# Layer 0 experts: owners loaded by fours, eight places for finished tiles, shared expert by four batches

## The chip, the cores and the metric

The kernel runs on one NeuronCore of a Trainium2 chip. The core has five engines that work side by side: TensorE (matrix products and transposes, PE in the rows; its weight loads are PEld), VectorE (DVE), ScalarE (ACT), GpSimd (POOL), and SyncE (SP), which issues most DMAs. TensorE reads SBUF and writes PSUM, eight banks of 128 x 512 floats; the other engines empty the banks. Engines wait for each other by semaphores. The metric is the time of one launch in microseconds of the device.

## What is computed

A decoder of four layers over 16 x 128 = 2048 tokens of width 256, each layer with attention, cross-attention and a feed-forward part. The change touches the feed-forward part of layer 0 alone, a mixture of 32 experts (inner width 128), of which each token takes 8, and a shared expert that all tokens take:

```python
aff = jax.nn.sigmoid(logits)
top_v, top_i = jax.lax.top_k(aff, K)
top_w = top_v / (jnp.sum(top_v, axis=-1, keepdims=True) + 1e-09)
...
shared = jnp.dot(silu(jnp.dot(x, Wg_s) + bg_s) * (jnp.dot(x, Wu_s) + bu_s), Wd_s) + bd_s
gate = silu(jnp.einsum('th,ehi->eti', x, Wg) + bg[:, None, :])
up = jnp.einsum('th,ehi->eti', x, Wu) + bu[:, None, :]
down = jnp.einsum('eti,eih->eth', gate * up, Wd) + bd[:, None, :]
routed = jnp.einsum('te,eth->th', w_full, down)
return (shared + routed).reshape(b, s, h)
```

## The kernel before

Only `l0_ffn` matters here. The 2048 tokens are 16 tiles of 128 rows, taken in three groups of 4, 8 and 4 tiles (`SIZES`). For each group the router finds for every token its 8 experts; GpSimd scatters the token's row 8 times into DRAM (`rows_dram`), sorted by expert and padded so that a tile of 128 rows holds rows of one expert only. That gives 63, 95 and 63 tiles, 221 in all (`ALL`). Which expert a tile belongs to, its owner, is known only at run time; a row `owner` in SBUF holds the numbers, and TensorE's sequencer loads them into registers (`values_load_multi_w_load_instructions`), since they address the expert's weights.

All engines then run one loop over units u, software-pipelined. SyncE reads tile m into one of four places of `tile_in`. `turn` (TensorE): two transposes of the tile; `copy` (ScalarE) brings them to `tileT`. `up`: a bias product and two products of 256 columns against the owner's gate and up weights, each fp32 product in two passes. `silu` on ScalarE, `multiply` on VectorE, `turn_hidden` (TensorE) transposes the hidden tile, `copy_hidden` (VectorE) brings it to `hiddenT`, `down` (TensorE) is one product of 256 columns. `take` (VectorE) copies the result to one of four places of `normed` (named `tile_out`), and SyncE writes that place to DRAM (`back_dram`). Before it uses a place, `take` waits for the semaphore `wrote` of the write four tiles earlier (line 2339); the copy itself (line 2340) waits for `downed`.

The order on TensorE in a round of u is turn(u + 3), up(u + 2), down(u), turn_hidden(u + 1). With every 24th tile (`BATCHED`), `turn` first loads the owners of the next 24 tiles (line 2109). VectorE's order is take(u), copy_hidden(u + 1), multiply(u + 2), and then what is due of `COMBINED`: when a token tile's 8 rows have come back by GpSimd's gathers (line 2050, gated by `out_taken`), VectorE adds them in 8 pieces, three to a unit (line 2360). That is done inside the loop for the 12 token tiles of groups 0 and 1; the last group is combined in a later stage.

The shared expert follows as 16 more units of the same loop, one for each token tile (`UNITS` = 16 + 221): a bias product (line 2130), two products with the tokens as stationary operand, silu, multiply, a transpose, a copy, a product of the routing weights with the experts' down biases (`bd`, line 2147) and the down product; VectorE adds the result to the tokens (line 2343). Then the next stage begins: its engines start, and SyncE issues its first loads, behind the end of this one.

Of the kernel before, what the change touches and what calls it, by code (L numbers as in the profile page):

```python
# [13 lines left out]
ALU = mybir.AluOpType  # L14
# [1833 lines left out]
def l0_ffn(k):  # L1848
# [15 lines left out]
    ALL = sum(TILES)  # L1864
    UNITS = BATCH + ALL
    BATCHED = 24
    rows_dram = k.routed
    back_dram = [nc.dram_tensor(f"expert_rows{g}", (TILES[g] * P, DIM), F32, kind="Internal").ap() for g in range(3)]
    k.last_rows = back_dram[2]
    with ExitStack() as stack:  # L1870
        wr, a = weights(k, stack, n + "Wr", KD, E)
        br, b = bias_row(k, stack, n + "br", E)
        bd = sb(k, stack, "bd", [P, DIM])
        shared_bias = sb(k, stack, "shared_bias", [P, DIM])
        before = sb(k, stack, "before", [P, P])
# [15 lines left out]
        xT = [k.xT, *(sb(k, stack, "xT", [P, KD, GT]) for _ in range(3))]  # L1891
        affinity, rest = sb(k, stack, "affinity", [P, 8, E]), sb(k, stack, "rest", [P, 8, E])
# [4 lines left out]
        mine, slots = sb(k, stack, "mine", [P, E * 8]), sb(k, stack, "slots", [P, E * 8])  # L1897
        is_it = sb(k, stack, "is_it", [P, GROUP * TOP, E])
# [10 lines left out]
        hiddenT = sb(k, stack, "hiddenT", [P, 2, INNER])  # L1909
        tile_out = k.normed  # L1910

# [17 lines left out]
        def out_bank(u):  # L1929
            return k.ps[:, 5 + u % 2, 0:DIM]  # L1930

        def turned_bank(m):
# [54 lines left out]
        with phase(k, "experts", names) as (block, s), ExitStack() as more:  # L1987
            for r in range(4):
                s[f"wrote{r}"] = more.enter_context(nc.semaphore(f"experts_wrote{r}"))
# [9 lines left out]
            def _(sp):  # L1999
# [6 lines left out]
                for m in range(ALL + 7):  # L2006
                    if m < ALL:
                        g = group_of(m)
                        if m == BEGIN[g]:
                            sp.wait_ge(k.scattered[g], 16 * TOP * SIZES[g])  # L2010
                        if m >= 4:
                            sp.wait_ge(s["tile_turned"], m - 3)
                        sp.dma_start(tile_in[:, m % 4, :], rows_dram[g][sl(m - BEGIN[g]), :]).then_inc(s[f"read{m % 4}"], 16)
                    if m >= 7:
                        j = m - 7
                        g = group_of(j)
                        sp.wait_ge(s["out_taken"], j + 1)
                        sp.dma_start(back_dram[g][sl(j - BEGIN[g]), :], tile_out[:, j % 4, :]).then_inc(s[f"wrote{j % 4}"], 16)
                for r in range(4):
                    sp.wait_ge(s[f"wrote{r}"], 16 * len(range(r, ALL, 4)))  # L2020

            @block.gpsimd
            def _(pool):
# [18 lines left out]
                for g in range(2):  # L2042
                    for r in range(4):
                        pool.wait_ge(s[f"wrote{r}"], 16 * len(range(r, BEGIN[g] + TILES[g], 4)))
                    for t in range(FIRST[g], FIRST[g] + SIZES[g]):
# [8 lines left out]
            def _(pe):  # L2054
# [41 lines left out]
                def weight(u, at, width):  # L2096
                    if not is_tile(u):
                        return experts[:, E, at:at + width]
                    return experts[:, bass.ds(expert_of[u], 1), at:at + width].rearrange("p o d -> p (o d)")

                def turn(m):
                    if m == 0:
                        for job in (("choose", 2), ("own", 1)):
                            job_taken(pe, job)
                    if m % BATCHED == 0:
                        count = min(BATCHED, ALL - m)
                        if m <= BEGIN[2] < m + count:
                            job_taken(pe, ("own", 2))
                        _, values = nc.values_load_multi_w_load_instructions(
                            owner[0:1, m:m + count], engines=[mybir.EngineType.PE], min_val=0, max_val=E - 1,  # L2110
                            skip_runtime_bounds_check_because="the owners are clamped to the last expert")
                        expert_of.update({m + j: value for j, value in enumerate(values)})
                    pe.wait_ge(s[f"read{m % 4}"], 16 * (m // 4 + 1))
# [6 lines left out]
                def up(u):  # L2120
                    if u >= 2:
                        pe.wait_ge(s["multiplied"], u - 1)
                    t = u - ALL
                    if is_tile(u):
                        if u == 0:
                            pe.wait_ge(s["weighted"], 16 * 5)
                        nc.tensor.matmul(gate_bank(u), one_hot[:, u:u + 1].broadcast_to([3 * E, P]), bias_parts[:, :], start=True, stop=False)
                        pe.wait_ge(s["tile_copied"], u + 1)
                    else:
                        nc.tensor.matmul(gate_bank(u), k.ident[:, 0:1].broadcast_to([P, P]), shared_bias[:, :], start=True, stop=False)  # L2130
                    for kt in range(KD):
                        x = tileT[:, u % 2, sl(kt)] if is_tile(u) else xT[t // GROUP][:, kt, sl(t % GROUP)]
                        last = nc.tensor.matmul(gate_bank(u), x, weight(u, 2 * kt * INNER, 2 * INNER), start=False, stop=kt == KD - 1)  # L2133
                    last.then_inc(s["upped"], 1)
# [7 lines left out]
                def down(u):  # L2142
                    if u >= 2:
                        pe.wait_ge(s["out_taken"], u - 1)
                    if not is_tile(u):
                        t = u - ALL
                        nc.tensor.matmul(out_bank(u), chosenT[t // GROUP][:, sl(t % GROUP)], bd[:, :], start=True, stop=False)
                    pe.wait_ge(s["hidden_copied"], u + 1)
                    nc.tensor.matmul(out_bank(u), hiddenT[:, u % 2, :], weight(u, 2 * KD * INNER, DIM), start=is_tile(u), stop=True).then_inc(s["downed"], 1)  # L2149

                for job in JOBS[:-7]:
                    make(job)
                for u in range(-3, UNITS):
# [5 lines left out]
                    if 0 <= u + 2 < UNITS:  # L2159
                        up(u + 2)  # L2160
                    if u >= 0:
                        down(u)
                    if 0 <= u + 1 < UNITS:
                        turn_hidden(u + 1)

            @block.scalar
            def _(act):
# [28 lines left out]
                def silu(u):  # L2196
# [11 lines left out]
                act.wait_ge(s["outered"], 1)  # L2208
                for u in range(-3, UNITS):
# [5 lines left out]
                    if 0 <= u + 2 < UNITS:  # L2215
                        silu(u + 2)

            @block.vector
            def _(dve):
# [115 lines left out]
                def take(u):  # L2335
                    dve.wait_ge(s["downed"], u + 1)
                    if is_tile(u):
# [3 lines left out]
                    else:  # L2341
                        t = u - ALL
                        v.tensor_tensor(k.x[:, t, :], out_bank(u), k.x[:, t, :], ALU.add).then_inc(s["out_taken"], 1)

# [41 lines left out]
                late = routing(2)  # L2386
                for u in range(-3, UNITS):
                    if u >= 0:
                        take(u)
                    if 0 <= u + 1 < UNITS:  # L2390
                        copy_hidden(u + 1)
                    if 0 <= u + 2 < UNITS:
                        multiply(u + 2)
                    if u in LATE_PIECES:
                        next(late, None)
                    for t, c in COMBINED.get(u, ()):
                        combine(t, c)
                for t in LEFT:
                    for c in range(TOP):
# [2531 lines left out]
def lay_out_rest(i, w):  # L4931
# [16 lines left out]
    w[n + "experts"] = np.concatenate([by_partition(np.concatenate([up, up_s[None]]), 2), down], axis=2).transpose(1, 0, 2)  # L4948
    w[n + "biases"], w[n + "shared_bias"] = np.tile(gate_and_up("b*", 1), (3, 1)), padded(row(gate_and_up("b*_s", 0)))
    w["numbers"] = np.broadcast_to(np.arange(32, dtype=np.float32), (P, 32))  # L4950
# [201 lines left out]
```

## Time and profile before

| | us |
|---|---|
| median of 3 runs (lowest, highest) | 3328.42 (3327.92, 3354.23) |
| span of the profiled execution | 3397.0 |
| tile loop of the layer 0 experts, first up to last up | 484.5 to 929.8 |
| shared expert, to the stage's last sum | to 970.8 |

The profile was taken in one execution of its own; its span is 68.6 us longer than the median run. In the rows below, a line such as L2133 is a line of the kernel before, `out<-in` are the program's names of what is written and read, `x4` is a count. A start and a duration stand in front; in square brackets stands how long the engine was idle before and what ended that. "issue" there means that nothing the profile shows was waited for. TensorE's matmuls overlap, and their ends are modelled: the pitch from start to start tells more than the duration.

### The profile page before, as it was taken

What the parts mean: (1) busy time and instruction counts of PE and PEld (TensorE: products, weight loads), DVE (VectorE), ACT (ScalarE), POOL (GpSimd) and SP (SyncE); (2) the same over time, 40 slices, a digit from 0 to 9 for tenths busy, and PEclk for the clock granted to TensorE, in tenths of its full rate; (3) what the DMA queues carried; (4) which work ended last, traced back from release to release, by engine and by line L of the source; (5) the groups of instructions that cost most, each with busy time, mean ns of one, the idle gap of its engine ahead of it and who ended that gap; (6) DMA issues with size and microseconds to landing.
All of it is one profiled execution on the core that took longest, in us unless ns stands there. A gap on an engine that the chain in (4) does not pass through costs nothing. (4 is left out here: it accounts for less than half of the span.)

```text
span 3397.0 us, 59298 instructions
## 1 busy us (share of the span) xinstructions
PE 3009.1 (89%) x20925; PEld 1857.6 (55%) x20929; DVE 2235.3 (66%) x4489; ACT 1822.0 (54%) x4182; POOL 1132.7 (33%) x1288
## 2 busy tenths in 40 slices
PE   7979759998887799987799989797799999999889
PEld 4656548877664556653467657454333333333567
DVE  6777645454546656667567747525589999996672
ACT  6967713333213344445566645211278888888554
POOL 3535555433432022215166653012111111221333
PEclk9999869999998999998889999898789999999989
DMA  9300156665530000022000032132401111110300
GB/s 301 133 9 2 47 203 210 207 188 173 158 101 26 26 1 1 1 73 85 33 1 1 1 118 106 64 109 88 113 1 20 20 21 20 21 20 1 125 13 25
DMA packets 158228, 243.61 MB, mean 72 GB/s; under 512 B 21298, under 2 KB 130482, under 8 KB 152482
## 3 DMA queue, kind: packets, MB, share of 16 engines
q1 hardware_dynamic: 144114, 202.05, 19.6%
q0 software_dynamic: 13824, 37.77, 3.4%
q8 instruction: 173, 2.83, 0.4%
q14 instruction: 117, 0.96, 0.1%
HBM read 132.64 MB, written 107.10 MB: 71 GB/s over the span
## 5 line engine op out<-in xcount | busy, mean ns | idle before, releaser
L4783 DVE TENSOR_REDUCE peaks<-ps 128x2 f32<-128x1024 f32 x512 | 617.6, 1219 | 64.8 <-PE ps L4727 63.0
L4820 ACT ACTIVATE attn<-ps 128x512 f32<-128x512 f32 x1024 | 558.8, 596 | 113.1 <-PE ps L4717 56.8
L4717 PE MATMUL ps<-queries,keys 50*128 50x512 f32 x1024 | 383.8, 455 | 0.0
L4727 PE MATMUL ps<-keys,queries 50*128 50x512 f32 x1024 | 370.2, 468 | 12.8 <-DVE peaks L4783 7.9
L4742 PE MATMUL ps<-attn,head_values 128*32 128x256 f32 x4096 | 332.3, 397 | 9.2 <-ACT output L4831 9.2
L4717 PEld LDWEIGHTS ps<-queries,keys 50*128 50x128 f32 x1024 | 157.6, 188 | 215.6 <-ACT attn L4820 197.5
L1239 POOL TENSOR_TENSOR attn_w<-attn_w,attn_share 128x512 f32<-128x512 f32 x128 | 131.7, 1050 | 373.0 <-DVE attn_share L1085 373.0
L2133 PE MATMUL ps<-experts,tileT 128*128 x884 | 232.0, 385 | 2.1 <-issue 2.1
L2340 DVE COPY normed<-ps 128x256 f32<-128x256 f32 x221 | 93.8, 424 | 202.9 <-PE ps L2149 106.8
L4742 PEld LDWEIGHTS ps<-attn,head_values 128*32 128x32 f32 x4096 | 82.3, 108 | 197.9 <-issue 108.6
L2194 ACT ACTIVATE tileT<-ps 128x256 f32<-128x256 f32 x221 | 84.6, 383 | 168.4 <-PE ps L2117 115.7
L2149 PE MATMUL ps<-experts,hiddenT 128*128 (+1 forms) x474 | 147.2, 392 | 25.1 <-DVE hiddenT L2349 21.1
L2133 PEld LDWEIGHTS ps<-experts,tileT 128*128 128x128 f32 x884 | 153.2, 193 | 19.4 <-issue 3.8
L4727 PEld LDWEIGHTS ps<-keys,queries 50*128 50x128 f32 x1024 | 147.5, 192 | 28.4 <-DVE peaks L4783 16.6
L2200 ACT ACTIVATE gate<-ps 128x128 f32<-128x128 f32 x237 | 65.8, 277 | 173.9 <-PE ps L2133 152.6
L1076 DVE TENSOR_REDUCE attn_peak<-ps 128x4 f32<-128x512 f32 x128 | 87.7, 685 | 95.9 <-PE ps L958 95.9
L4870 POOL CAST peak_parts<-peak 128x8 fp32r<-128x8 f32 x32 | 6.3, 197 | 407.4 <-DVE peak L4789 387.8
L2050 POOL DMA_INDIRECT rows<-expert_rows,index x96 | 91.0, 948 | 150.2 <-DMA expert_rows<-normed 60.9
L972 PE MATMUL ps<-xT,L_xattn_Wq 128*128 128x512 f32 x256 | 124.7, 610 | 7.7 <-ACT qT L1176 6.2
L2038 POOL DMA_INDIRECT routed_rows<-rows,index x96 | 96.3, 1003 | 87.7 <-DVE normed L2340 61.5
L2149 PEld LDWEIGHTS ps<-experts,hiddenT 128*128 128x128 f32 x474 | 86.8, 191 | 52.8 <-issue 41.1
L4885 POOL CAST queries<-peak_rows 2x128 fp32r<-2x128 f32 x256 | 73.5, 287 | 125.3 <-DVE peak_rows L4795 111.6
(733 smaller groups left out, 7164.5 us busy)
## 6 DMA issues: line engine op xcount, KB each, us to landing
tile_in<-routed_rows SPq DMA_DIRECT2D x244, 128.0 KB, 2.2
expert_rows<-normed SPq DMA_DIRECT2D x221, 128.0 KB
routed_rows<-zeros SPq DMA_DIRECT2D x2, 8064.0 KB, 48.1
experts<-in_L_ffn_experts SPq DMA_DIRECT2D x4, 3072.0 KB
routed_rows<-zeros SPq DMA_DIRECT2D x1, 12160.0 KB, 67.0
kT<-L_xattn_keys SPq DMA_DIRECT2D x8, 1024.0 KB
v<-L_xattn_values SPq DMA_DIRECT2D x8, 1024.0 KB, 8.7
experts<-in_L_ffn_experts SPq DMA_DIRECT2D x8, 1024.0 KB
```

The lines of the kernel that those rows point to most:

```text
L972: last = nc.tensor.matmul(query_bank, wq[:, kt, sl(4 * p + jj)], xT[g % 2][:, kt, :], start=kt == 0, stop=kt == KD - 1)
L1239: nc.gpsimd.tensor_tensor(w, w, share[:, n % 2, side, :].unsqueeze(2).broadcast_to([P, 4, P]), ALU.mult).then_inc(s_["scaled"], 1)
L2038: nc.gpsimd.indirect_dma_start(rows_dram[g][:, :], bass.IndirectOffsetOnAxis(index_of(slice(t, t + 1))[:, 0, c:c + 1], 0), rows[:, t, :], ...
L2050: nc.gpsimd.indirect_dma_start(rows[:, TOP * (t % 2) + c, :], None, back_dram[g][:, :], bass.IndirectOffsetOnAxis(index[:, t, c:c + 1], 0) ...
L2133: last = nc.tensor.matmul(gate_bank(u), x, weight(u, 2 * kt * INNER, 2 * INNER), start=False, stop=kt == KD - 1)
L2149: nc.tensor.matmul(out_bank(u), hiddenT[:, u % 2, :], weight(u, 2 * KD * INNER, DIM), start=is_tile(u), stop=True).then_inc(s["downed"], 1)
L2340: v.tensor_copy(tile_out[:, u % 4, :], out_bank(u)).then_inc(s["out_taken"], 1)
L4717: nc.tensor.matmul(bank(("score", n)), keys[pair % 2][rows, sl(kt)], queries[pair % 2][rows, sl(c, CHUNK)], start=True, stop=True).then_in ...
L4727: last = nc.tensor.matmul(k.ps[:, SB + p % PB, :], queries[pair % 2][rows, sl(t)], keys[pair % 2][rows, sl(c, CHUNK)], start=True, stop=True)
L4742: last = nc.tensor.matmul(mixed_bank[sl(strip, PAD), columns], head_values[:, u // CHUNKS % 2, strip % 2, 2 * part + strip // 2, :], attn[ ...
L4783: v.tensor_reduce(peaks[:, r % 2, i // CHUNKS, :, i % CHUNKS], k.ps[:, at:at + 2, :], AX.X, ALU.max).then_inc(s["maxed"], 1)
L4820: nc.scalar.activation(attn[:, n % RING, :], bank(("score", n)), ACT.Exp, scale=1.0 / 16.0).then_inc(s["read"], 1)
```

## The change

Three things are changed in `l0_ffn`.

Owners are loaded four at a time (`LOADED`), 56 loads for 221 tiles. The first stands ahead of the loop, each further one behind `down(u)`, for the tiles u + 4 to u + 7, and no longer in `turn`.

From tile 64 on (`WIDE`) finished tiles go to eight places in turn: the four of `normed` and four in the storage of `is_it`, which the router no longer needs by then. `take` then waits for the write eight tiles earlier. There are eight `wrote` semaphores.

The shared expert leaves the loop. It runs as four batches of 512 tokens, with the weights as stationary operand and the tokens streaming through, 512 columns at a time. The result is the hidden tile already transposed, so `turn_hidden` and `copy_hidden` fall away; a bias is now one value for each partition and enters in the silu and in VectorE's multiply. `shared_up(0)` stands ahead of the loop's last but one `down`, and `shared_up(i + 1)` ahead of the downs of batch i.

```diff
-    UNITS = BATCH + ALL
-    BATCHED = 24
+    LOADED = 4
+    WIDE = 64
...
-        tile_out = k.normed
+        outs = is_it[:, :, :].rearrange("p a e -> p (a e)")
+        shared_gate = [tile_in[:, 0:2, :].rearrange("p a d -> p (a d)"), ranked[:, :, :].rearrange("p a e -> p (a e)")]
+        shared_hiddenT = [tile_in[:, 2:4, :].rearrange("p a d -> p (a d)"), affinities[:, :, :, :].rearrange("p a t e -> p (a t e)")]
+
+        def tile_out(u):
+            return outs[:, sl(u % 4, DIM)] if u >= WIDE and u % 8 >= 4 else k.normed[:, u % 4, :]
+
+        def out_before(u):
+            return u - 8 if u >= WIDE + 8 else u - 4 if u < WIDE + 4 else -1
+
+        def written(engine, u):
+            engine.wait_ge(s[f"wrote{u % 8}"], 16 * (u // 8 + 1))
...
+                def owners(m):
+                    count = min(LOADED, ALL - m)
+                    if m <= BEGIN[2] < m + count:
+                        job_taken(pe, ("own", 2))
+                    _, values = nc.values_load_multi_w_load_instructions(
+                        owner[0:1, m:m + count], engines=[mybir.EngineType.PE], min_val=0, max_val=E - 1,
+                        skip_runtime_bounds_check_because="the owners are clamped to the last expert")
...
-                    if m % BATCHED == 0:
-                        count = min(BATCHED, ALL - m)
-                        if m <= BEGIN[2] < m + count:
-                            job_taken(pe, ("own", 2))
...
+                def shared_up(i):
+                    if i == 1:
+                        pe.wait_ge(s["multiplied"], ALL)
+                    if i >= 2:
+                        pe.wait_ge(s["shared_multiplied"], i - 1)
+                    for half in range(2):
+                        for kt in range(KD):
+                            last = nc.tensor.matmul(shared_bank(i, half), experts[:, E, sl(2 * kt + half)], xT[i][:, kt, :], start=kt == 0, stop=kt == KD - 1)
+                    last.then_inc(s["shared_upped"], 1)
+
+                def shared_down(t):
+                    pe.wait_ge(s["out_taken"], ALL + t - 1)
+                    out = out_bank(ALL + t)
+                    nc.tensor.matmul(out, chosenT[t // GROUP][:, sl(t % GROUP)], bd[:, :], start=True, stop=False)
+                    pe.wait_ge(s["shared_multiplied"], t // GROUP + 1)
+                    nc.tensor.matmul(out, shared_hiddenT[t // GROUP % 2][:, sl(t % GROUP)], experts[:, E, 2 * KD * INNER:COLS],
+                                     start=False, stop=True).then_inc(s["downed"], 1)
...
+                    if u == ALL - 2:
+                        shared_up(0)
                     if u >= 0:
                         down(u)
-                    if 0 <= u + 1 < UNITS:
+                    if is_tile(u + 4) and (u + 4) % LOADED == 0:
+                        owners(u + 4)
+                    if is_tile(u + 1):
                         turn_hidden(u + 1)
+                for i in range(GROUPS):
+                    if i + 1 < GROUPS:
+                        shared_up(i + 1)
+                    for t in range(GROUP * i, GROUP * i + GROUP):
+                        shared_down(t)
...
+                def shared_silu(i):
+                    act.wait_ge(s["shared_upped"], i + 1)
+                    if i >= 2:
+                        act.wait_ge(s["shared_multiplied"], i - 1)
+                    nc.scalar.activation(shared_gate[i % 2], shared_bank(i, 0), ACT.Silu, bias=shared_bias[:, 0:1]).then_inc(s["shared_silued"], 1)
...
-                        if u >= 4:
-                            dve.wait_ge(s[f"wrote{u % 4}"], 16 * (u // 4))
-                        v.tensor_copy(tile_out[:, u % 4, :], out_bank(u)).then_inc(s["out_taken"], 1)
...
+                    if out_before(u) >= 0:
+                        written(dve, out_before(u))
+                    v.tensor_copy(tile_out(u), out_bank(u)).then_inc(s["out_taken"], 1)
+
+                def shared_multiply(i):
+                    dve.wait_ge(s["shared_silued"], i + 1)
+                    if i >= 2:
+                        dve.wait_ge(s["downed"], ALL + GROUP * (i - 1))
+                    v.scalar_tensor_tensor(shared_hiddenT[i % 2], shared_bank(i, 1), shared_bias[:, 1:2], shared_gate[i % 2],
+                                           ALU.add, ALU.mult).then_inc(s["shared_multiplied"], 1)
...
+                shared_multiply(0)
+                shared_multiply(1)
+                for i in range(GROUPS):
+                    for t in range(GROUP * i, GROUP * i + GROUP):
+                        shared_take(t)
+                    if i + 2 < GROUPS:
+                        shared_multiply(i + 2)
```

On TensorE, around a load of owners in the middle of the loop, before (ISA is the step that computes a weight's address from the owner's register; `tile_in`, `tileT`, `hidden` and `hiddenT` are the tile and its hidden form, plain and transposed):

```order
L2149 MATMUL ps<-experts,hiddenT 128x256
L2140 MATMUL ps<-ident,hidden 128x128
L2109 TENSOR_LOAD owner
L2117 MATMUL ps<-ident,tile_in 128x128 x2
L2127 MATMUL ps<-bias_parts,one_hot 128x256
L2133 ISA
L2133 MATMUL ps<-experts,tileT 128x256
```

and in the changed kernel, at each fourth tile:

```order
L2157 MATMUL ps<-experts,hiddenT 128x256
L2121 TENSOR_LOAD owner
L2151 MATMUL ps<-ident,hidden 128x128
L2133 MATMUL ps<-ident,tile_in 128x128 x2
L2141 MATMUL ps<-bias_parts,one_hot 128x256
L2144 ISA
L2144 MATMUL ps<-experts,tileT 128x256
```

The load has moved from behind the hidden transpose to between the down product and that transpose.

On TensorE, one unit of the shared expert before (`xT` are the transposed tokens, `chosenT` the transposed routing weights):

```order
L2140 MATMUL ps<-ident,hidden 128x128
L2130 MATMUL ps<-shared_bias,ident 128x256
L2133 MATMUL ps<-experts,xT 128x256 x2
L2147 MATMUL ps<-bd,chosenT 128x256
L2149 MATMUL ps<-experts,hiddenT 128x256
```

and in the changed kernel from the loop's last hidden transpose on, with the first of the sixteen pairs of down (`tile_in` now holds the hidden tile of a batch):

```order
L2166 MATMUL ps<-xT,experts 128x512 x4
L2157 ISA
L2157 MATMUL ps<-experts,hiddenT 128x256
L2151 MATMUL ps<-ident,hidden 128x128
...
L2166 MATMUL ps<-xT,experts 128x512 x4
L2172 MATMUL ps<-bd,chosenT 128x256
L2174 MATMUL ps<-experts,tile_in 128x256
```

The bias products and the hidden transposes of the shared units are gone, and the ups stand in front of the downs by fours.

## Rows read from the trace of the kernel before

**Rows 1.** The head of the profile's page.
```profile
span 3397.0 us, 59298 instructions
```
**Rows 2.** Busy us (instructions) of PE, PEld, DVE, ACT, POOL, PEclk, DMA; then up (L2133).
```profile
520.00:800.00 280.00, 269.23 (x1524) 228.19 (x1523) 146.59 (x513) 100.19 (x304) 104.47 (x110) 1.00 0.63 194
800.00:936.00 136.00, 111.64 (x570) 87.96 (x569) 75.96 (x236) 34.81 (x112) 60.70 (x64) 0.96 0.57 168
...
L2133 PE MATMUL ps<-experts,tileT x884: 377/378/787, 484.5 to 930.5; 128*128 x177
```
**Rows 3.** Timeline of TensorE, a tile and then a load of owners: start, us, line.
```profile
578.26 1.03 PE L2133 MATMUL ps<-experts,tileT 128*128 x4
579.13 0.59 PE L2149 MATMUL ps<-experts,hiddenT 128*128 x2
579.56 0.27 PE L2140 MATMUL ps<-ident,hidden 128*128 128x128 f32 x1
...
580.00 1.03 PE L2133 MATMUL ps<-experts,tileT 128*128 x4
...
581.29 0.27 PE L2140 MATMUL ps<-ident,hidden 128*128 128x128 f32 x1
582.81 0.41 PE L2117 MATMUL ps<-ident,tile_in 128*128 128x128 f32 x2 [1.24 <-issue]
```
**Rows 4.** Waits of the stage: who waited for what; us in total, times, longest.
```profile
DVE normed L2340 <- remote: 21.8, 6, 3.9
...
PE ps L2117 <- issue: 10.3, 8, 1.5
```
**Rows 5.** Loads of owners: ns least/median/most, first and last start; all, two singly.
```profile
L2109 PEldq TENSOR_LOAD <-owner x10: 696/1864/2047, 463.5 to 919.5; - x10
...
L2109 PEldq TENSOR_LOAD <-owner x1: 1867/1867/1867, 580.8 to 580.8; - x1
...
L2109 PEldq TENSOR_LOAD <-owner x1: 696/696/696, 919.5 to 919.5; - x1
```
**Rows 6.** VectorE's waits for a place (L2339), all, then from 878 to 884.
```profile
L2339 DVEq EVENT_SEMAPHORE  x217: 21/21/2027, 501.4 to 934.2; - x109
...
L2339 DVEq EVENT_SEMAPHORE  x1: 21/21/21, 879.0 to 879.0; - x1
```
**Rows 7.** Timeline of that stall.
```profile
879.39 0.69 PE L2149 MATMUL ps<-experts,hiddenT 128*128 x2 [0.53 <-issue]
...
880.78 0.95 POOL L2050 DMA_INDIRECT rows<-expert_rows,index  x1 [0.30 <-issue]
...
880.99 0.38 ACT L2194 ACTIVATE tileT<-ps 128x256 f32<-128x256 f32 x1 [3.55 <-PE ps L2117]
...
883.22 0.42 DVE L2340 COPY normed<-ps 128x256 f32<-128x256 f32 x1 [3.87 <-remote]
```
**Rows 8.** Timeline of the last tile's up and of the end of the shared expert.
```profile
929.81 1.03 PE L2133 MATMUL ps<-experts,tileT 128*128 x4
...
968.24 0.70 PE L2149 MATMUL ps<-experts,hiddenT 128*128 128x256 f32 x2 [0.17 <-DVE hiddenT L2349]
...
969.65 0.70 PE L2149 MATMUL ps<-experts,hiddenT 128*128 128x256 f32 x2 [0.17 <-DVE hiddenT L2349]
970.39 0.42 DVE L2343 TENSOR_TENSOR x<-ps,x 128x256 f32<-128x256 f32 x1 [0.79 <-PE ps L2149]
```
**Rows 9.** Timeline of TensorE behind the load of five owners at 919.5.
```profile
920.50 0.27 PE L2140 MATMUL ps<-ident,hidden 128*128 128x128 f32 x1
920.61 0.38 PE L2117 MATMUL ps<-ident,tile_in 128*128 128x128 f32 x2
```
**Rows 10.** Like shapes elsewhere: 512-column passes, a multiply (busy, mean ns), a ScalarE function.
```profile
977.86 3.67 PE L3250 MATMUL ps<-xT,L_attn_W_q 128*128 128x512 f32 x8 [0.83 <-ACT xT L3320]
...
L3788 DVE SCALAR_TENSOR_TENSOR rows<-ps,factor,gate 128x512 f32<-128x512 f32 x32 | 23.1, 747 | 6.9 <-ACT gate L3724 5.2 <-PE ps L3678 0.7
...
L4820 ACT ACTIVATE attn<-ps 128x512 f32<-128x512 f32 x1024 | 558.8, 596 | 113.1 <-PE ps L4717 56.8
```

More of the change, by code:

```diff
@@ L1930, in out_bank, with shared_bank @@
             return k.ps[:, 5 + u % 2, 0:DIM]
+        def shared_bank(i, half):
+            return k.ps[:, 2 * (i % 2) + half, :]
         def turned_bank(m):
@@ L1987, in l0_ffn @@
         with phase(k, "experts", names) as (block, s), ExitStack() as more:
-            for r in range(4):
+            for m in ("shared_upped", "shared_silued", "shared_multiplied"):
+                s[m] = more.enter_context(nc.semaphore(f"experts_{m}"))
+            for r in range(8):
                 s[f"wrote{r}"] = more.enter_context(nc.semaphore(f"experts_wrote{r}"))
@@ L2042, in _ @@
                 for g in range(2):
-                    for r in range(4):
-                        pool.wait_ge(s[f"wrote{r}"], 16 * len(range(r, BEGIN[g] + TILES[g], 4)))
+                    for u in range(BEGIN[g + 1] - 8, BEGIN[g + 1]):
+                        written(pool, u)
                     for t in range(FIRST[g], FIRST[g] + SIZES[g]):
@@ L2096, in weight @@
                 def weight(u, at, width):
-                    if not is_tile(u):
-                        return experts[:, E, at:at + width]
                     return experts[:, bass.ds(expert_of[u], 1), at:at + width].rearrange("p o d -> p (o d)")
+                def owners(m):
[5 more added lines that the diff above has]
+                        skip_runtime_bounds_check_because="the owners are clamped to the last expert")
+                    expert_of.update({m + j: value for j, value in enumerate(values)})
                 def turn(m):
                     if m == 0:
-                        for job in (("choose", 2), ("own", 1)):
-                            job_taken(pe, job)
-                    if m % BATCHED == 0:
-                        count = min(BATCHED, ALL - m)
-                        if m <= BEGIN[2] < m + count:
-                            job_taken(pe, ("own", 2))
[L2109 to L2112, printed above, removed]
+                        job_taken(pe, ("choose", 2))
                     pe.wait_ge(s[f"read{m % 4}"], 16 * (m // 4 + 1))
@@ L2144, in down @@
                         pe.wait_ge(s["out_taken"], u - 1)
-                    if not is_tile(u):
-                        t = u - ALL
-                        nc.tensor.matmul(out_bank(u), chosenT[t // GROUP][:, sl(t % GROUP)], bd[:, :], start=True, stop=False)
                     pe.wait_ge(s["hidden_copied"], u + 1)
-                    nc.tensor.matmul(out_bank(u), hiddenT[:, u % 2, :], weight(u, 2 * KD * INNER, DIM), start=is_tile(u), stop=True).then_inc(s["downed"], 1)
+                    nc.tensor.matmul(out_bank(u), hiddenT[:, u % 2, :], weight(u, 2 * KD * INNER, DIM), start=True, stop=True).then_inc(s["downed"], 1)
+                def shared_up(i):
[14 more added lines that the diff above has]
+                                     start=False, stop=True).then_inc(s["downed"], 1)
                 for job in JOBS[:-7]:
                     make(job)
-                for u in range(-3, UNITS):
+                job_taken(pe, ("own", 1))
+                owners(0)
+                for u in range(-3, ALL):
                     for job in LATE:
@@ L2208, in _ @@
                 act.wait_ge(s["outered"], 1)
-                for u in range(-3, UNITS):
+                for u in range(-3, ALL):
                     for job in LATE:
@@ L2386, in _ @@
                 late = routing(2)
-                for u in range(-3, UNITS):
+                for u in range(-3, ALL):
                     if u >= 0:
                         take(u)
-                    if 0 <= u + 1 < UNITS:
+                    if is_tile(u + 1):
                         copy_hidden(u + 1)
-                    if 0 <= u + 2 < UNITS:
+                    if is_tile(u + 2):
                         multiply(u + 2)
@@ L4948, in lay_out_rest @@
     w[n + "experts"] = np.concatenate([by_partition(np.concatenate([up, up_s[None]]), 2), down], axis=2).transpose(1, 0, 2)
-    w[n + "biases"], w[n + "shared_bias"] = np.tile(gate_and_up("b*", 1), (3, 1)), padded(row(gate_and_up("b*_s", 0)))
+    w[n + "biases"], w[n + "shared_bias"] = np.tile(gate_and_up("b*", 1), (3, 1)), columns(gate_and_up("b*_s", 0))
     w["numbers"] = np.broadcast_to(np.arange(32, dtype=np.float32), (P, 32))
```

42 lines of the change are left out of this document (20 added, 22 removed).

## The prediction

> **What bounds the kernel now.** The change lies in one stage, the experts of layer 0, so I read that stage and not the shares of the whole span. The table by stretches comes first [rows 2]: from 520 to 800 us TensorE is busy 269.2 of 280 us at a granted clock of 1.00 (2.4 GHz), VectorE 146.6, ScalarE 100.2. TensorE bounds the tile loop. From 800 to 936 us it is busy 111.6 of 136, idle 24.4, at a clock of 0.96.
>
> The timeline of a tile is next [rows 3]: a row of TensorE work without a hole. Up starts at 578.26 and the next up at 580.00, 1.74 us later; four passes of up take 0.87 of it and two of down 0.43. From the first up (484.5) to the last (929.8) the loop takes 445.3 us [rows 2, 8], where 220 steps of 1.74 are 382.8. 62.5 us are lost; the change aims at two pieces of that, and at the shared expert.
>
> First piece: the load of owners. The eight waits on "issue" that TensorE's transposes of new tiles have sum to 10.3 us [rows 4], one for each of the eight loads of 24 values inside the loop. In the timeline the transposes start 1.52 us behind the hidden transpose (581.29 to 582.81) [rows 3]; without a load it is 0.11 (920.50 to 920.61) [rows 9]. A load costs 1.41, eight cost 11.3.
>
> Second piece: the copy of a finished tile to its place. The table of waits says that VectorE waited 21.8 us for "remote" ahead of that copy, in 6 waits [rows 4]. It reads like places that their writes have not left. But the instruction that waits for the place stands at L2339, apart from the copy: its median over 217 is 21 ns, and inside a stall of 3.87 us, at 879.0, it took 21 ns too [rows 6]. What came late there was TensorE's signal: down started at 879.39 and lasted 0.69, the copy began at 883.22; and ScalarE's copy of a turned tile, which waits for TensorE and for no place, is late in the same moments (idle 3.55) [rows 7]. GpSimd's gathers stand back to back beside it, 0.30 us apart. More places do not shorten that.
>
> Third piece: the shared expert, from the last tile's up (929.81) to the end of the last sum (970.39 + 0.42 = 970.81), 41.0 us [rows 8].
>
> **The change, part by part.**
>
> *Owners by fours.* Removed: 11.3 us, from above. Added: 55 loads inside the loop. Four values were never loaded; five took 696 ns and 24, in the load of [rows 3], 1867 (median 1864) [rows 5]. That is 62 ns for each further value, so four take 0.63 us. What of it shows depends on the work that is issued already. In [rows 3] the load starts at 580.8 [rows 5] and the issued work lasts until 581.4 (hidden transpose at 581.29 and 0.11): 0.6 us are covered. The load ends at 582.65, the next transpose starts at 582.81: 0.15 to start again. The new place is one step earlier, ahead of the hidden transpose; 0.11 less work is issued by then, but the load is reached about one step sooner, so I keep 0.6. Shown: 0.63 + 0.15 - 0.6 = 0.18 us. The load of five at 919.5 speaks for less: the transposes behind it follow at 920.61 without a hole [rows 9]. Of the 55 I take 45 as exposed; the others fall in tiles where VectorE holds TensorE up anyway (12 token tiles are combined inside the loop, each over three units). 45 x 0.18 = 8.1 us, and the edit is worth -11.3 + 8.1 = -3.2. Bounds: all covered, -11.3; nothing covered, 55 x 0.78 = 42.9, so +31.6. I stay at the low end because the nearest row, five values, shows no hole.
>
> A page of the Trainium skill speaks against this edit: "DMA: Bandwidth & Descriptors", section "Latency and other measured facts", gives a register load a floor of about 600 ns and says that loads are unrolled by four to spread it. The five-value row (696 ns) agrees. By the page, with each floor bare, 55 x 0.6 = 33 us would come in and the time would be 3342 us, an estimate; by the rows the issued work hides most of each load, and bare loads are a rival below.
>
> *Eight places from tile 64 on.* Removed: waits that take 21 ns. Worth 0. What covers them is the lag of four tiles, some 7 us, between a write and the reuse of its place; were a write later than that, each tile would wait for the rest. The write, its place in SyncE's queue and GpSimd's waits for a group's writes remain, under other semaphores. Bounds: 0, up to all that is lost from 800 to 936: 24.4 idle less two loads (2.8), and 4% of the clock (5.4), 27 us.
>
> *Shared expert.* Before: 41.0 us, as above. After, from the same up, on TensorE: up 0.86, down 0.43, hidden transpose 0.11, together 1.40. The first shared up. Down 0.43, transpose 0.11, the last down's wait for its hidden copy 0.87 (968.24 + 0.43 to 969.65 is 0.98 [rows 8], with a transpose of 0.11 in it), down 0.43, together 1.84. Three more shared ups. 16 pairs of down at 0.86, 13.8. The tail to the last sum 0.73 (969.65 + 0.43 to 970.81). A shared up is four products of 512 columns, eight passes; the nearest row has the same shape in the next stage, eight in 3.67 us [rows 10], at most 0.46 each with the modelled end of the last one in it; twice a pass of 256 columns (0.43 for two [rows 3]) is 0.43, and I take that: 3.44 an up, 13.8 for four. VectorE multiplies batches 1 to 3 ahead of the sums of the batch before. A signal of TensorE acts after 0.31 (969.65 + 0.43 to 970.39), a silu takes 0.60 on 512 columns, a multiply 0.75 [rows 10], the sum 0.42: with 0.05 between, the first sum ends 2.15 us behind a shared up, while TensorE wants its bank again after two pairs, 1.72. 0.43 is lost, three times: 1.3. Sum: 1.40 + 13.8 + 1.84 + 13.8 + 1.3 + 0.73 = 32.9 us. Gone are the bias product, the hidden transpose and the hidden copy of 16 units. Worth 32.9 - 41.0 = -8.1. Bounds: no wait, -9.4; silu and multiply bare behind all four ups (4 x 1.7 for 1.3), -2.6.
>
> *Sum.* -3.2 + 0 - 8.1 = -11.3 us. The profiled execution has a span of 3397.0 us [rows 1], 68.6 above the median of the runs (3328.42); no row says in which stage that lies. Against its own span the forecast is 3385.7, and the same 11.3 off the median is 3317.1 us. The next stage begins where this one ends (SyncE issues its first loads only then), so it moves by as much.
>
> **Rivals.**
>
> *The places matter (faster).* If the late signals come from traffic that the reuse of places keeps in step, loosening it could free the 27 us: 3290.1. For it: the stalls lie where gathers stand back to back. Against it: 21 ns at L2339 in the stall [rows 6], and ScalarE late as well [rows 7].
>
> *Bare loads (slower).* If a load is reached only when the array has run dry, each of 55 shows 0.63 + 0.15: -11.3 + 42.9 - 8.1 = +23.5, 3351.9. For it: down, right ahead of the load, waits for the hidden copy, so issue cannot run far ahead, and where that copy is late only down's own 0.43 covers. Against it: [rows 9]. It decides from 0.35 shown per load on ((11.3 + 8.1) / 55); below that the kernel is still faster.
>
> *Shared batches in single file.* Each batch pays silu and multiply bare: -2.6 for -8.1, 3322.6. Against it: the next batch's up is issued ahead of the downs of the one before.
>
> **How the numbers follow.** Forecast, with the single file inside it, 0.70; its own range is 3308 to 3330 (loads from all covered to 0.3 shown, the shared part between its bounds). Places 0.14. Bare loads 0.09. Something that no row shows 0.07. About 1% (33 us) is what a measurement of this kernel can tell from no change, and the forecast is within it. The places' case (3290.1) is just over it and makes, with a part of the unknown, the 0.16 for faster; bare loads end within it, so slower has 0.05 and the same 0.79. The range goes down to 3288 to hold the places, and up to 3338 to hold loads of which a good half is bare; outside stay the fully bare loads and the unknown.
>
> **What would show each step.** Right: 56 loads of some 0.63 us on TensorE's queue, holes under 0.25 us ahead of the hidden transpose, steps of 1.74 between; the wait for a place at 21 ns before and after tile 64; the stalls of some 3 us still there beside the gathers; the last tile's up to the last sum in 32 to 34 us, 512-column passes 0.43 apart. Wrong: four values take well over 0.7, or the hole is near 0.4; the stalls beside the gathers are gone; or this stage is shorter and a later one has grown by as much.

## The result, and the profile after

| | us |
|---|---|
| before, median of 8 runs (lowest, highest) | 3332.04 (3323.68, 3354.23) |
| changed, median of 8 runs (lowest, highest) | 3311.65 (3303.84, 3319.88) |
| ratio, 95% interval | 0.9929, 0.9912 to 0.9946 |
| forecast, range | 3317.1, 3288 to 3338 |

The changed kernel takes 20.4 us less between the medians, 0.6%, and 0.7% less by the ratio: within 1%, as forecast, and the interval leaves no doubt of the sign. The forecast was a gain of 11.3 us.

The profiled execution of the changed kernel took 3306.56 us, in line with its timed runs. Its span, 3304.7 us, is 92.3 us shorter than the one that [rows 1] shows, over four times what the timed runs give. The execution behind [rows 1 to 10] was a long one of its kernel, so I compare with a second profile of the kernel before, taken later, and come back to the first below.

The stage of the changed kernel by stretches (stretch, length, then busy us and instructions of PE, PEld, DVE, ACT, POOL; PEclk, DMA share, GB/s), the answer to [rows 2]:

```profile
520.00:800.00 280.00, 277.44 (x1583) 236.75 (x1582) 149.62 (x523) 104.35 (x315) 112.56 (x118) 1.00 0.65 203
800.00:884.00 84.00, 80.47 (x441) 65.02 (x440) 62.94 (x193) 29.12 (x88) 49.29 (x51) 1.00 0.74 218
```

From 520 to 800 us TensorE is idle 2.6 us, where it was 10.8 [rows 2]; behind 800 the clock is 1.00 and 3.5 of 84 us are idle. The tiles' up products now run from 477.2 to 883.9, 406.6 us.

The loads of owners (ns least/median/most, first and last start), and one of them singly, the answer to [rows 5]:

```profile
L2121 PEldq TENSOR_LOAD <-owner x56: 305/333/520, 453.9 to 880.8; - x56
...
L2121 PEldq TENSOR_LOAD <-owner x1: 332/332/332, 626.5 to 626.5; - x1
```

TensorE's timeline around that one (start, us, line), the answer to [rows 3]:

```profile
625.79 1.03 PE L2144 MATMUL ps<-experts,tileT 128*128 x4
626.65 0.59 PE L2157 MATMUL ps<-experts,hiddenT 128*128 x2
627.09 0.27 PE L2151 MATMUL ps<-ident,hidden 128*128 128x128 f32 x1
...
627.53 1.03 PE L2144 MATMUL ps<-experts,tileT 128*128 x4
```

A load of four takes 333 ns, not 630. It starts at 626.5, beside the products of down, and is over at 626.86; the hidden transpose follows down after 0.44 us and the next up after 1.74: no hole. In TensorE's waits of the stage the "issue" ahead of the transposes of new tiles, 10.3 us in [rows 4], is gone (who waited for what: us, times, longest):

```profile
PE ps L2157 <- DVE hiddenT L2401: 5.7, 16, 0.8
PE ps L2157 <- issue: 1.6, 10, 0.2
PE ps L2172 <- DVE x L2395: 0.2, 1, 0.2
```

The end of the stage, the answer to [rows 8]: the last tile's up, the first two shared ups, a bubble, the last down and the last sum.

```profile
883.86 1.03 PE L2144 MATMUL ps<-experts,tileT 128*128 x4
885.39 0.69 PE L2157 MATMUL ps<-experts,hiddenT 128*128 x2 [0.51 <-DVE hiddenT L2401]
...
886.03 3.60 PE L2166 MATMUL ps<-xT,experts 128*128 128x512 f32 x8
889.47 0.59 PE L2157 MATMUL ps<-experts,hiddenT 128*128 x2
...
890.97 0.69 PE L2157 MATMUL ps<-experts,hiddenT 128*128 x2 [0.80 <-DVE hiddenT L2401]
891.50 3.60 PE L2166 MATMUL ps<-xT,experts 128*128 128x512 f32 x8
...
896.23 0.59 PE L2174 MATMUL ps<-experts,tile_in 128*128 128x256 f32 x2
897.00 0.70 PE L2172 MATMUL ps<-bd,chosenT 128*128 128x256 f32 x2 [0.17 <-DVE x L2395]
...
916.50 0.59 PE L2174 MATMUL ps<-experts,affinities 128*128 128x256 f32 x2
917.13 0.42 DVE L2395 TENSOR_TENSOR x<-ps,x 128x256 f32<-128x256 f32 x1 [0.44 <-PE ps L2174]
```

From 883.86 to 917.55 are 33.7 us, for 41.0 before and 32.9 forecast.

### The profile page after: what moved, and what is told of

Same layout as the page of the kernel before. It is cut to its first block and busy times, and to the rows that moved or that the text cites. A ratio compares the mean times of both kernels' runs of the same rounds, so it can differ in the third digit from the quotient of the medians.

```text
span 3304.7 us, 59090 instructions
## 1 busy us (share of the span) xinstructions
PE 2969.0 (90%) x20849; PEld 1829.3 (55%) x20849; DVE 2226.6 (67%) x4461; ACT 1823.7 (55%) x4170; POOL 1133.1 (34%) x1288
## 5 line engine op out<-in xcount | busy, mean ns | idle before, releaser
L2157 PE MATMUL ps<-experts,hiddenT 128*128 x442 | 134.8, 387 | 7.4 <-DVE hiddenT L2401 5.7
L2384 DVE COPY normed<-ps 128x256 f32<-128x256 f32 x144 | 61.1, 424 | 117.1 <-PE ps L2157 114.6
L4322 POOL TENSOR_TENSOR lasting<-lasting,pairs 128x512 f32<-128x512 f32 x64 | 81.1, 1281 | 82.0 <-ACT lasting L4247 82.0
```

## The experiments

**A second profile of the kernel before.** No edit.

> The kernel before, unchanged, profiled a second time. In the profile shown, its tiles take 445.3 us from the first tile's up products to the last tile's, 38.7 us more than in the changed kernel's profile, of which only about 11 us are holes at the loads of the owners; the rest are some ten stalls of about 3 us in tiles 160 to 215. Theory A (the stalls were the profiled execution's own, not the kernel's): this profile has the tiles in 415 to 420 us, a span about 3310 to 3330 us, the stretch 800 to 936 us without stalls, and the holes at loads again: 1.9 us nine times, 0.7 us once. Rival B (the four places for finished tiles make the stalls): 440 to 447 us of tiles again, with some eight to ten stalls of about 3 us after tile 160.

Its span is 3321.2 us. The stage in two stretches (columns as above):

```profile
520.00:800.00 280.00, 268.03 (x1514) 228.34 (x1512) 143.06 (x500) 99.91 (x302) 104.93 (x110) 0.99 0.62 193
800.00:892.00 92.00, 86.91 (x478) 70.66 (x477) 65.54 (x203) 31.31 (x95) 53.73 (x56) 1.00 0.73 216
```

Its loads, and VectorE's waits for a place, all and then those from 541.9 us on (columns as in [rows 5, 6]):

```profile
L2109 PEldq TENSOR_LOAD <-owner x10: 825/1860/2042, 454.7 to 881.7; - x10
...
L2339 DVEq EVENT_SEMAPHORE  x217: 21/21/3560, 488.0 to 896.3; - x109
...
L2339 DVEq EVENT_SEMAPHORE  x192: 21/21/50, 541.9 to 896.3; - x192
```

The tiles take 416.3 us, not 445.3. The holes at the loads are all there: steps from up to up of 4.16, 3.45, 3.34, 3.22, 3.11, 3.04, 3.05, 3.73 us at the loads of 24 and 2.84 at the load of five. The 60 steps from tile 160 on take 114.7 us, for 139.8 in the first profile and 111.7 in the changed kernel's. So the stalls of [rows 7] belong to that execution and do not come with the kernel each time: theory A. Of the 75.8 us between the two spans only 29.0 lie in the tile loop; 8.8 lie ahead of it and 38.0 behind the stage. Why that one execution was so long stays open.

**Each part alone.** Owners by fours; eight places; the shared expert by batches, each edit by itself. The first two were put into the kernel before; for the third the other two were set back in the changed kernel (loads of 24 ahead of a turn, `WIDE = 1000`):

```diff
-                    if m % BATCHED == 0:
-                        count = min(BATCHED, ALL - m)
...
+                    if is_tile(u + 4) and (u + 4) % LOADED == 0:
+                        owners(u + 4)
```
```diff
+            return outs[:, sl(u % 4, DIM)] if u >= WIDE and u % 8 >= 4 else k.normed[:, u % 4, :]
```
```diff
+                for i in range(GROUPS):
+                    if i + 1 < GROUPS:
+                        shared_up(i + 1)
+                    for t in range(GROUP * i, GROUP * i + GROUP):
+                        shared_down(t)
```

> The kernel before with one part of the change: the owners are read four at a time behind a down product instead of 24 at a time ahead of a turn; four places and the shared expert tile by tile stay. The changed kernel's trace has 56 loads of 333 ns in the middle, all but the first ahead of an idle-free stretch. Theory A (loads are covered): the 11.3 us of holes go and nothing comes in their place: -11 us, -10 to -13. The predicted sum (a load of four takes 0.63 us, 0.18 us of it shown) would give -3 us. Rival B (bare loads): 56 x 0.33 us = 18.5 us come for 18.6 us of loads gone, so 0 to +7 us.

> The kernel before with one part of the change: eight places for finished tiles from tile 64 on. Theory A (VectorE never waited for a place, 21 ns each in the trace): 0 us, within -2 to +2, and a profile whose tiles take as long as in a second profile of the kernel before. Rival B (the stalls of tiles 160 to 215 are waits for a place): -20 to -27 us, and no stall left in the stretch 800 to 936 us.

> The kernel before with one part of the change: the shared expert by four batches of 512 columns; the owners are read by 24 ahead of a turn and finished tiles have four places, as before. Theory A (the predicted step): the stage end after the last tile's up products falls from 41.0 to 33 or 34 us, -7 to -8 us in the time. Rival B (the batches go in single file): 38 to 39 us, -2 to -3 us. If the other two parts give -11 and 0, all three together give -18 to -20 us, which is what the changed kernel shows in time (-20.4 us between the medians).

The table has the ratios of time, and two lengths from the timeline of each profile: from the start of tile 10's up to the start of tile 220's (the first ten steps are left out, since in equal code they came to 22 to 28 us), and from there to the end of the stage's last sum.

| | ratio to before, 95% interval | tiles 10 to 220, us | behind them, us |
|---|---|---|---|
| before, second profile | | 393.4 | 41.0 |
| owners alone | 0.9962, 0.9945 to 0.9978 | 379.9 | 41.0 |
| places alone | 1.0004, 0.9987 to 1.0021 | 393.5 | 41.0 |
| shared expert alone | 0.9982, 0.9967 to 0.9998 | 394.0 | 33.7 |
| changed kernel | 0.9929, 0.9912 to 0.9946 | 379.8 | 33.7 |
| changed, second time | 0.9932, 0.9908 to 0.9956 | 379.8 | 33.7 |
| changed, four places | 0.9931, 0.9911 to 0.9952 | 380.1 | 33.7 |
| changed, fours in `turn` | 0.9919, 0.9901 to 0.9938 | 380.8 | 33.7 |

Owners: 393.4 - 379.9 = 13.5 us, of which 12.4 lie in the nine steps with a load; of the rest, 1.5 lie in the step behind the first load (3.23 us): TensorE had been idle 1.5 us at that load, and then the granted clock was 0.50, the level of 1.2 GHz (524 to 527 us). In time it is -12.7 us. Shared expert: 7.3; -6.0 in time. Places: nothing; +1.3 in time, within its interval. The sum by profiles, -20.8, is close to what the two medians give (-20.4). The ratios add up less closely: -17.4 for the parts and -23.7 for the whole, 6.3 us apart, where each ratio is known to 5 or 6 us either way.

**Without the places; and fours where the 24 stood.** `WIDE = 1000` in the changed kernel, and, separately, its loads put back into `turn`:

```diff
+                    if m and m % LOADED == 0:
+                        owners(m)
...
-                    if is_tile(u + 4) and (u + 4) % LOADED == 0:
-                        owners(u + 4)
```

> The changed kernel without one part: four places for finished tiles throughout, the owners by fours and the shared expert by batches as changed. Theory A (the places carry nothing, also once the loads are off the path): as the changed kernel, whose ratio is 0.9929; the sum of the two parts measured alone, -12.7 and -6.0 us, is -18.7 us or 0.9944; so 0.993 to 0.995, and tiles that take 406 to 408 us. Rival B (a place starts to be waited for when the tiles come without holes): 4 to 5 us less gained, 0.9955 or more, and waits for finished tiles' rows in VectorE's list of over 21 ns each.

> The changed kernel with the owners' loads, still four at a time, put back ahead of a turn, where the load of 24 stood. In the kernel before, a load of 24 took 1.86 us there and lengthened a tile's step by 1.31 to 1.5 us, so about 0.4 to 0.5 us of it lay beside other work. Theory A (size alone hides a load): 0.33 us is less than that, the steps at loads stay at 1.74 us, tiles take 406 to 408 us, ratio as the changed kernel's. Rival B (the place matters, a load ahead of a turn shows whole): 55 x 0.33 = 18 us come back, the steps at loads are 2.07 us, ratio about 0.9985.

Four places are as fast as eight, and the fours cost at most 1 us in the old position (380.8 for 379.8), nothing in time: theory A both times. The loads of the second kernel, in `turn`:

```profile
L2121 PEldq TENSOR_LOAD <-owner x56: 330/376/562, 454.4 to 879.1; - x56
```

At 376 ns they still lie beside issued work. The gain of the edit is the size of the load; its place gave 1 us at most.

**The price of a load, and its cover.** The changed kernel, with loads of other lengths behind `down`:

```diff
-                    count = min(LOADED, ALL - m)
+                    count = LENGTHS[m]
```

> The changed kernel with the owners read in loads of 4, 1, 2, 3, 5, 6, 7, 8, 12 and 16 values in turn, each behind a down product; it prices the load and its cover. Theory A (a load costs about 311 ns for each begun four values, as 24 values at 1864 ns, 5 at 696, 4 at 333 and 1 at 305 suggest): 1 to 4 values 0.31 to 0.33 us, 5 to 8 values 0.62 to 0.70 us, 12 values 0.93, 16 values 1.24 us. Rival B (a line through 5 and 24 values, as predicted: 61.5 ns a value and 0.39 us ahead): 1 value 0.45, 4 values 0.63, 8 values 0.88, 12 values 1.13, 16 values 1.37 us. A step of 1.74 us stays so while the load is under some 0.5 us; 12 values lengthen it by about 0.4 us, 16 values by about 0.7 us.

> The changed kernel with the owners read in loads of 5, 3, 6, 2, 7, 1, 2, 4, 8 and 2 values in turn, so that 5, 6, 7 and 2 start at a multiple of four values in the list, while 4 and 8 start two beyond one. In the run with other lengths, loads of 4, 8, 12 and 16 that started at a multiple of four took about 0.3 us for each four values (0.33, 0.60 to 0.84, 0.95 to 1.11, 1.20 to 1.31 us), while 2, 3, 5, 6 and 7 that started elsewhere took about 0.3 us for each value (5 values 1.38 to 1.70 us); the last load of the kernel before, 5 values from a multiple of four, took 0.70 us. Theory A (the start decides: from a multiple of four a load takes 0.3 us for each four values and for each of the rest, from elsewhere 0.3 us for each value): 5 from a multiple 0.65 to 0.75 us, 6 0.9 to 1.1, 7 1.2 to 1.4; 4 from elsewhere 1.1 to 1.35 us, 8 from elsewhere 2.2 to 2.6 us. Rival B (the length decides, not the start): 5, 6 and 7 again 1.4 to 2.2 us, 4 again 0.33 us, 8 again 0.6 to 0.85 us. In both, a step grows by the load's time less about 0.42 us.

Four loads of the first kernel (8, 16, 7 and 5 values; the 8 and the 16 start at a multiple of four in the list):

```profile
L2127 PEldq TENSOR_LOAD <-owner x1: 598/598/598, 777.7 to 777.7; - x1
...
L2127 PEldq TENSOR_LOAD <-owner x1: 1210/1210/1210, 813.3 to 813.3; - x1
...
L2127 PEldq TENSOR_LOAD <-owner x1: 1862/1862/1862, 764.1 to 764.1; - x1
...
L2127 PEldq TENSOR_LOAD <-owner x1: 1375/1375/1375, 863.6 to 863.6; - x1
```

TensorE's timeline around the 7:

```profile
764.23 0.59 PE L2163 MATMUL ps<-experts,hiddenT 128*128 x2
766.13 0.30 PE L2157 MATMUL ps<-ident,hidden 128*128 128x128 f32 x1 [1.31 <-issue]
```

Three of the second (6 from a multiple of four; 4 and 8 from two beyond one):

```profile
L2127 PEldq TENSOR_LOAD <-owner x1: 1021/1021/1021, 804.2 to 804.2; - x1
...
L2127 PEldq TENSOR_LOAD <-owner x1: 1139/1139/1139, 682.8 to 682.8; - x1
...
L2127 PEldq TENSOR_LOAD <-owner x1: 2168/2168/2168, 690.5 to 690.5; - x1
```

TensorE's timeline around the 6:

```profile
804.35 0.59 PE L2163 MATMUL ps<-experts,hiddenT 128*128 x2
805.37 0.30 PE L2157 MATMUL ps<-ident,hidden 128*128 128x128 f32 x1 [0.42 <-issue]
```

The first run's theory A was half right: it left out the start. From a multiple of four a load costs some 0.3 us for each four values (8: 0.60 to 0.84; 12: 0.95 to 1.11; 16: 1.20 to 1.31) and some 0.3 for each value left over (5: 0.60 to 1.07; 6: 0.83 to 1.13; 7: 1.17 to 1.30). From elsewhere it costs about 0.3 for each value: 4 took 1.12 to 1.33, 8 took 2.17 to 2.70. Seven values cost 1.17 to 1.30 us or 1.86 to 2.28, by their start. The second run's theory A holds in the main, with wider spreads than it gave, and the rival, that length alone decides, fell. One length does not fit: two values took 0.78 to 1.00 us from a multiple of four, and 0.53 to 0.78 from two beyond one. Why the start matters stays open. With these lengths tiles 10 to 220 took 400.2 us (first run) and 411.4 (second), longer than with loads of 24 (393.4).

The cover is in the two timelines. Behind the load of six the transpose starts 1.02 us after down instead of 0.43: 0.59 are shown of 1.02. Behind the load of seven it is 1.90 - 0.43 = 1.47 of 1.86. So about 0.4 us of a load is hidden here, and one of 0.33 us vanishes.

**What still holds the tiles back.** In the changed kernel most steps are 1.74 us, but eleven pairs are some 0.95 us too long. The timeline of VectorE and TensorE around one of them:

```profile
837.14 1.53 DVE L2412 SCALAR_TENSOR_TENSOR x<-rows,share,x 128x256 f32<-128x256 f32 x3
837.28 0.69 PE L2157 MATMUL ps<-experts,hiddenT 128*128 x2 [0.16 <-issue]
...
838.71 0.42 DVE L2384 COPY normed<-ps 128x256 f32<-128x256 f32 x1
...
839.45 1.00 DVE L2412 SCALAR_TENSOR_TENSOR x<-rows,share,x 128x256 f32<-128x256 f32 x2
839.58 0.69 PE L2157 MATMUL ps<-experts,hiddenT 128*128 x2 [0.30 <-DVE hiddenT L2401]
```

Three additions take 1.53 us, the copies behind them are late, and down waits for `hiddenT`. Two runs spread the additions, the first of them two tiles sooner:

```diff
-                        COMBINED.setdefault(at + c // 3, []).append((t, c))
+                        COMBINED.setdefault(at - 2 + (c if g == 0 else c * 3 // 4), []).append((t, c))
```

> The changed kernel with one other edit, to look for what still holds the tiles back: in the changed kernel's trace most steps are 1.74 us, but eleven times a pair of steps is 2.15 and 2.3 us, together about 0.95 us too long, where VectorE adds three weighted rows (485 ns each) behind one tile, while its own work for a tile is 0.98 of 1.74 us. Here the additions go one behind each tile (eight tiles), or in the second group eight behind six tiles, and begin two tiles sooner. Theory A (three additions at once are the cause): 7 to 10 us less than the changed kernel, ratio to the kernel before about 0.990, tiles in 397 to 400 us. Rival B (the gathers on GpSimd, 1.25 us each and eight in six tiles, set these steps, or the rows land too late for additions two tiles sooner): 0 or some us slower, with waits of VectorE for rows.

> The even additions again, but in the second group they begin where they began in the changed kernel, not two tiles sooner: in the run with the sooner start, VectorE waited for the rows five times (5.8 us in all, once 2.4 us) and a step grew to 4.13 us. Theory A (the additions were too early, their evenness is right): the steps of 3.18 and 4.13 us go; tiles 10 to 220 take 369 to 372 us, against 374.9 with the sooner start and 379.8 in the changed kernel; 8 to 10 us less than the changed kernel run beside it. Rival B (the rows have two sets of places, and additions that end later hold up the next gathers, so the rows are late again): 374 to 378 us, with VectorE's waits for rows again, and no gain beyond 5 us.

> The changed kernel, unchanged, on the same chip and beside the run above, for a comparison without other chips between, and for a second profile. If the account by parts holds: ratio to the kernel before 0.992 to 0.995, tiles 10 to 220 in 379 to 381 us, 33.2 us from the last tile's up products to the stage's last product, loads of four 333 ns and steps of 1.74 us at them, no stalls of 3 us among tiles 160 to 215.

Tiles 10 to 220 took 374.9 us with the sooner start and 372.7 with the later one, for 379.8. The pairs are gone, but in the second group the rows now come late. The timeline of the worst place of the first run, and then VectorE's wait for rows in the first and in the second (us, times, longest):

```profile
821.82 1.01 DVE L2412 SCALAR_TENSOR_TENSOR x<-rows,share,x 128x256 f32<-128x256 f32 x2 [2.40 <-DMA rows<-expert_rows,index]
...
823.74 0.69 PE L2157 MATMUL ps<-experts,hiddenT 128*128 x2 [2.13 <-DVE hiddenT L2401]
```
```profile
DVE x L2412 <- DMA rows<-expert_rows,index: 5.8, 5, 2.4
```
```profile
DVE x L2412 <- DMA rows<-expert_rows,index: 3.8, 6, 1.2
```

Both theories hold in part. The pairs are worth some 10 us (eleven of 0.95), an estimate, and 4.9 and 7.1 came. The gathers now wait longer for VectorE's additions (16.9 and 18.6 us, for 10.4 in the changed kernel), and VectorE's waits for late rows, 5.8 and 3.8 us, are about what is missing. In time the ratios are 0.9922 (0.9906 to 0.9938) and 0.9912 (0.9882 to 0.9942), beside 0.9932 (0.9908 to 0.9956) for the changed kernel run with the latter. That is no faster kernel that the runs could tell from the changed one.

## Why the prediction was right, and where it was off

**Owners by fours: the mechanism right, one term mis-sized.** The holes went (11.3 us by [rows 3, 4, 9], 13.5 measured, 2.2 beyond the bound that I gave: the second profile has a hole at the load of five too, and the slow step behind the first load). The cover was right: 0.6 us from the load's start, less 0.15 to start again, is 0.45; the two timelines above give 0.39 and 0.43. The step that failed is "62 ns for each further value, so four take 0.63 us". It drew a line through two points of a staircase: 24 values are six fours (1.86 us), five are a four and one (0.70 us). Four take 0.333 us, and 0.33 + 0.15 - 0.6 is below nothing. With that the predicted 8.1 us of new holes are 0, and the sum -11.3 + 0 - 8.1 = -19.4, next to the 20.4 measured.

The five-value row without a hole, which kept me at the low end, was a lucky guide. TensorE had been busy only 2.4 of the 5 us from 910 on, and the granted clock was 0.50 (1.2 GHz) from 917 to 919 us. From the load's start at 919.5 the issued work lasted to 920.61, some 1.1 us instead of the 0.6 of [rows 3]. In the second profile, at a clock of 1.00 (2.4 GHz), the load of five left a hole: the transposes started 0.61 us behind the hidden one, not 0.11. The stretch of the first profile (columns as in [rows 2]), then the load and TensorE's timeline in the second:

```profile
917.00:919.00 2.00, 2.00 (x8) 1.56 (x7) 1.89 (x6) 0.28 (x1) 0.87 (x1) 0.50 0.59 176
```

```profile
L2109 PEldq TENSOR_LOAD <-owner x1: 825/825/825, 881.7 to 881.7; - x1
...
882.11 0.27 PE L2140 MATMUL ps<-ident,hidden 128*128 128x128 f32 x1
882.72 0.41 PE L2117 MATMUL ps<-ident,tile_in 128*128 128x128 f32 x2 [0.34 <-issue]
```

The rule that I weighed against this edit was the floor of about 600 ns for a register load (the Trainium skill, "DMA: Bandwidth & Descriptors", section "Latency and other measured facts"). The trace disagrees: one value took 305 ns and four 333 ns. The section also names an unrolling by four; in these runs four values from a multiple of four cost about what one costs (333 and 305 ns). The estimate by the floor, 3342 us, is 30 us too long.

**Eight places: right.** 0 forecast; +1.3 us within its interval alone, and nothing taken away with them. The wait reads 21 ns (median) with four places and with eight. The median was not the whole of [rows 6], though, whose longest wait is 2027 ns. In the first profile eleven waits were longer than 0.1 us, 10.9 us in all: five by tile 23, which places from tile 64 on cannot touch, and six of 0.35 to 0.96 in the stalls. In the second profile only the first five are left; from 541.9 us on none is over 50 ns. So the forecast of 0 holds for the kernel, and the 21 ns in one stall spoke for less than I took from it.

**The stalls beside the gathers: a wrong reading of what belongs to the kernel.** I wrote that they would still be there; they are not, and the second profile of before has none. That did not reach the sum, since no term rested on them, but it did reach the rival (27 us, 0.14) and the low end of the range. The gap of 68.6 us between the span and the median was the warning: a stretch that only such an execution shows should have had no price.

**Shared expert: right within 1 us.** 33.7 for 32.9. The shared up is 3.44 us (886.03 to 889.47), as forecast. Ahead of the first one 2.17 us passed for 1.40, mostly since the down before it waited 0.51 for `hiddenT`; between the first two 2.03 for 1.84. The bubbles at a batch's third pair cost 0.34 each (896.23 to 897.00, less 0.43), 1.0 in all for 1.3.

**The rivals.** Bare loads did not come: the load stands beside down's own products, and even loads of 1.0 us showed only 0.6. Single file did not come: the next shared up is issued ahead, and of the batches' waits only VectorE's bubble is left.

**Range and chances.** The measured time lies 5.5 us below the forecast, inside the main case's own range, and "within 1%" came. The gain was missed by more, 20.4 for 11.3: the median of the kernel before rose by 3.6 us between the 3 runs that I had and the 8, which brought the times closer by chance. Nearly all of the miss is the owners' term.

## What to carry to other kernels

Price a load into registers by a row of its own length and start: here it went in pieces of four from a multiple of four, and a line between two other lengths doubled it. A hole at a bulk load vanishes when the pieces are shorter than the work that is already issued; where in the round they stand then matters little. Set a profile's span against the timed runs before pricing any stall in it, and profile the same kernel twice where they differ by more than the change is worth.

## What the runs showed of the hardware

The start of a register load counts beside its length: four values cost 0.33 us (median) from a multiple of four, and 1.12 to 1.33 us from two beyond one; eight cost 0.60 to 0.84 or 2.17 to 2.70. Two executions of one kernel differed by 29 us in one stage (tiles in 416.3 and 445.3 us) with the same instructions.
